# Low modes of 64 images: the table becomes the stationary operand and the images stream; one reload moves ahead of the last stores

## The reference, cut to what matters

```
xa_n = _inorm(xa, norm1_w, norm1_b)
k = _spec_conv(xa_n, kw1, kw2, (hk, wk))      # rfft2, 8x8 modes top and bottom, irfft2
q = _spec_conv(xa_n, qw1, qw2, (hk, wk))
v = _spec_conv(xa_n, vw1, vw2, (H, W))
dprod = softmax(einsum('batd,basd->bats', q, k) * sqrt(hk * wk))
att = einsum('bats,basd->batd', dprod, v)
att = _inorm(att, an_w, an_b) + xa
mix = _spec_conv(_inorm(att), mix_w1, mix_w2, (H, W))
```

## Time and profile before

| | us |
|---|---|
| median of 3 runs (lowest to highest) | 677.81 (675.39 to 679.09) |
| the profiled execution's own time | 681.9 |
| its span, first to last instruction | 679.9 |
| TensorE busy | 636.5 |
| VectorE busy | 487.8 |
| ScalarE busy | 334.3 |
| GpSimd busy | 356.1 |
| granted TensorE clock, mean | 0.984 of 2.4 GHz |

### The profile page before, as it was taken

How to read it: one execution, slowest core, us unless ns; L and a number is a source line. 1 busy time by engine, 2 the same in 40 slices (tenths; PEclk the granted TensorE clock), 3 DMA queues, 4 the chain that set the end, 5 groups by cost and what they waited for, 6 DMA issues and landing times.

```text
span 679.9 us, 15103 instructions
## 1 busy us (share of the span) xinstructions
PE 636.5 (94%) x5736; PEld 581.6 (86%) x5736; DVE 487.8 (72%) x1099; ACT 334.3 (49%) x722; POOL 356.1 (52%) x430
## 2 busy tenths in 40 slices
PE   9999999899999799979999899989999989995984
PEld 9999998699999799869999789969899988994863
DVE  4667676688777567668777666857887666778896
ACT  6888142465666413255666523246566650433331
POOL 0350035959960013796993002398799000359995
PEclk9999999899999899999999999999999989999997
DMA  9990000998999200299999900059989960004786
GB/s 320 350 379 9 1 2 20 308 314 294 310 318 328 94 1 1 77 308 343 286 328 309 322 14 1 2 198 331 321 285 325 308 218 1 1 1 162 280 302 247
DMA packets 72071, 136.32 MB, mean 200 GB/s; under 512 B 5760, under 2 KB 6272, under 8 KB 72000
## 3 DMA queue, kind: packets, MB, share of 16 engines
q1 hardware_dynamic: 72000, 135.36, 58.5%
HBM read 68.23 MB, written 67.11 MB: 199 GB/s over the span
## 4 chain that ended last, share of the span: by engine, by line
PE 58%; DVE 15%; POOL 9%; DMA 8%; issue 3%; ACT 3%; SPq 3%; POOLq 0%; DVEq 0%; ACTq 0%
PE psY L350 23%; PE psP L404 12%; POOL X L784 7%; PE psY L373 6%; DMA X<-in_x 6%; PE psT L389 5%; PE psP L454 5%; DVE QP L872 4%; ACT SQ L554 2%; PE psP L373 2%; DVE Y L836 2%; DVE SQ L836 2%; DMA out<-X 2%; SPq L318 2%; DVE X L836 1%
## 5 line engine op out<-in xcount | busy, mean ns | idle before, releaser
L350 PE MATMUL psY<-FWD,X 128*128 128x128 f32 x2048 | 251.1, 281 | 17.5 <-DMA X<-in_x 17.4
L350 PEld LDWEIGHTS psY<-FWD,X 128*128 128x128 f32 x2048 | 238.8, 195 | 33.0 <-issue 33.0
L784 POOL TENSOR_TENSOR X<-X,ALPHA 128x512 f32<-128x512 f32 x244 | 254.7, 1080 | 21.7 <-DVE IM L1072 19.7
L872 DVE TENSOR_REDUCE QP<-SQ 128x32 f32<-128x512 f32 x256 | 162.1, 679 | 57.8 <-ACT SQ L554 57.8
L836 DVE TENSOR_TENSOR X<-X,psP 128x512 f32<-128x512 f32 x192 | 126.5, 684 | 59.9 <-PE psP L404 26.1
L554 ACT ACTIVATE SQ<-X 128x512 f32<-128x512 f32 x256 | 146.4, 622 | 21.1 <-DMA X<-in_x 14.4
L404 PE MATMUL psP<-INVW,T 64*128 64x256 f32 x768 | 141.3, 402 | 12.0 <-DVE X L836 11.3
L762 POOL TENSOR_TENSOR Y<-Y,OMEGA 128x256 f32<-128x256 f32 x32 | 25.3, 790 | 215.9 <-ACT Y L558 215.6
L404 PEld LDWEIGHTS psP<-INVW,T 64*128 64x128 f32 x768 | 92.9, 190 | 31.2 <-issue 16.0
L576 ACT ACTIVATE T<-psT,BIA,SCL 128x256 f32<-128x256 f32 x128 | 65.3, 560 | 110.3 <-PE psT L389 105.8
L546 ACT ACTIVATE Y<-psY 128x512 f32<-128x512 f32 x128 | 76.2, 596 | 60.4 <-PE psY L350 59.6
(11 more groups left out here) (189 smaller groups left out, 478.8 us busy)
## 6 DMA issues: line engine op xcount, KB each, us to landing
X<-in_x SPq DMA_DIRECT2D x116, 512.0 KB, 5.5
out<-X SPq DMA_DIRECT2D x116, 512.0 KB, 4.4
X<-in_x SPq DMA_DIRECT2D x24, 256.0 KB, 5.2
out<-X SPq DMA_DIRECT2D x24, 256.0 KB, 3.7
INVH<-t_inv_h SPq DMA_DIRECT2D x1, 256.0 KB, 9.6
LW<-in_low_w SPq DMA_DIRECT2D x1, 204.0 KB, 6.6
GWT<-t_w SPq DMA_DIRECT2D x1, 192.0 KB, 9.9
FWD<-t_fwd SPq DMA_DIRECT2D x1, 128.0 KB, 2.1
```

Source lines behind the costliest of these rows:

```text
L350: last = mm(psY[p % 2][:, (2 * i + c) * 128:(2 * i + c + 1) * 128], X[:, 2 * p + i, a, c * 128:(c + 1) * 128], FWD[:, a, :], start=a == 0, ...
L784: P.tensor_tensor(v, v, al, MUL).then_inc(x_scaled, 1)
L872: V.tensor_reduce(QP[:, 4 * (k % 2) + place(n) % 4, :], SQ[:, n % RING, :].rearrange("p (a g j) -> p g a j", a=HC, j=GW), AX.XY, ADD).then ...
```

## The change

**Low modes.** For both k, the 64 columns of the table are now the stationary operand and 64 images times 8 values of u stream past it: 512 columns in one matmul, four matmuls (c, k), summed over c. k = 0 is written to partitions 0 to 63 and k = 1 to partitions 64 to 127 of one bank. u = 0 takes two matmuls of 64 columns. The result now has the table's columns on partitions, so it has to be turned: ScalarE copies it to SBUF (`ZT`, 128 by 512, and `ZT0`, 64 by 64), and nine matmuls with the copies as stationary operand and a new table MIRROR of ones, minus ones and zeros (32 columns) bring the images back on partitions and at the same time form the sums and differences for u and -u. The new table picks only the 8 values of v that are used. `modes(b, 0)` is split in two: its first half runs before the nine matmuls, its second half after them. VectorE then needs three plain copies instead of a copy, a copy, a sum and a difference. On ScalarE the two copies stand between the roots L600 and L602.

**SP's queue.** The reload of pair 29 now stands between the stores of pair 30 and of pair 31, and the reload of pair 30 comes right behind the stores of pair 31.

**Tables.** One more small table is loaded (16 KB), so 16 instead of 15 are counted.

```diff
@@ tables()
+    mirror = (row % 64 // 32 == col % 16 // 8) * (row % 32 == col % 8) * np.where(row // 64 * (col // 16) == 1, -1.0, 1.0)
@@ buffers
+        ZT, ZT0 = SQ[:, 0, :], SQ[0:64, 1, 0:IMGS]
@@ sync, batch(b, more)
-                for q in range(PAIRS - 2):
+                for q in range(PAIRS):
                     store(b, q)
                     if more and q:
                         reload(b + 1, q - 1)
-                for q in range(PAIRS - 2, PAIRS):
-                    store(b, q)
-                for q in range(PAIRS - 3, PAIRS) if more else ():
-                    reload(b + 1, q)
+                if more:
+                    reload(b + 1, PAIRS - 1)
@@ tensor, attend(b)
                 pe.wait_ge(scaled_w, 4 * b + 2)
-                for k, n in [(0, n) for n in range(1, 9)] + [(1, n) for n in range(1, 9)] + [(0, 0)]:
-                    ps, col = psZ[k if n else 2], 64 * max(n - 1, 0)
-                    if n == 0:
-                        pe.wait_ge(scaled_w, 4 * b + 4)
-                    for c in range(WC):
-                        last = mm(ps[0:IMGS, col:col + 64], Y[:, c, k, :, U0 + n], GWR[:, c, 0, k:k + 2, :],
-                                  start=c == 0, stop=c == WC - 1)
-                last.then_inc(z_made, 1)
-                modes(b, 0)
+                for c in range(WC):
+                    for k in range(2):
+                        last = mm(psZ[0][64 * k:64 * k + 64, :], GWR[:, c, 0, k:k + 2, :].rearrange("p r v -> p (r v)"),
+                                  Y[:, c, k, :, U0 + 1:U0 + 9], start=c == 0, stop=c == WC - 1)
+                last.then_inc(z_raw, 1)
+                pe.wait_ge(scaled_w, 4 * b + 4)
+                for c in range(WC):
+                    last = mm(psZ[1][0:64, 0:IMGS], GWR[:, c, 0, 0:2, :].rearrange("p r v -> p (r v)"),
+                              Y[:, c, 0, :, U0], start=c == 0, stop=c == WC - 1)
+                last.then_inc(z_raw, 1)
+                modes(b, 0, (0,))
+
+                pe.wait_ge(z_kept, 2 * b + 2)
+                for n in range(8):
+                    mm(psZ[2][0:IMGS, 32 * n:32 * (n + 1)], ZT[:, 64 * n:64 * (n + 1)], MIRROR[:, :],
+                       start=True, stop=True)
+                mm(psZ[2][0:IMGS, 256:272], ZT0, MIRROR[0:64, 0:16], start=True, stop=True).then_inc(z_made, 1)
+                modes(b, 0, (1,))
                 modes(b, 1)
@@ scalar, attend(b), between the roots L600 and L602
+                act.wait_ge(z_raw, 2 * b + 1)
+                nc.scalar.activation(ZT.rearrange("p (n i) -> p n i", n=8),
+                                     psZ[0][:, :].rearrange("p (i n) -> p n i", n=8), ACT.Copy).then_inc(z_kept, 1)
+                act.wait_ge(z_raw, 2 * b + 2)
+                nc.scalar.activation(ZT0, psZ[1][0:64, 0:IMGS], ACT.Copy).then_inc(z_kept, 1)
@@ vector, attend(b)
-                step(V.tensor_copy(sine, low_z(psZ[1], 8)))
-                do(V.tensor_copy(Xv[:, :, 8, :], low_z(psZ[2], 1)[:, 0, :, :]))
-                do(tt(Xv[:, :, 9:17, :], turned(low_z(psZ[0], 8)), turned(sine), ADD))
-                do(tt(Xv[:, :, 7::-1, :], turned(low_z(psZ[0], 8)), turned(sine), SUB))
+                low_z = psZ[2][0:IMGS, 0:256].rearrange("p (u s r v) -> p s r u v", s=2, r=2, v=LV)
+                do(V.tensor_copy(Xv[:, :, 8, :], psZ[2][0:IMGS, 256:272].rearrange("p (r v) -> p r v", r=2)))
+                do(V.tensor_copy(Xv[:, :, 9:17, :], low_z[:, 0, :, :, :]))
+                do(V.tensor_copy(Xv[:, :, 7::-1, :], low_z[:, 1, :, :, :]))
```

More of the change, by code:

```diff
@@ L15 @@
 PAIRS, QUADS, NG = IMGS // 2, IMGS // 4, IMGS // 8
-TABLES = 15
+TABLES = 16
 LAG = 3
@@ L68, in tables @@
                     + [p // 32 == i for i in range(4)], 1)
+    row, col = p[:, None], np.arange(32)[None, :]
+    mirror = (row % 64 // 32 == col % 16 // 8) * (row % 32 == col % 8) * np.where(row // 64 * (col // 16) == 1, -1.0, 1.0)
     f = lambda t: np.ascontiguousarray(t.reshape(t.shape[0], -1).astype(np.float32))
@@ L71, in tables @@
             "t_group": f(group_of), "t_eye": f(np.eye(IMGS)), "t_side": f(side), "t_pair": f(pair),
-            "t_rows": f(rows), "t_sel": f(p[:, None] % GROUPS == np.arange(GROUPS)[None, :])}
+            "t_mirror": f(mirror), "t_rows": f(rows), "t_sel": f(p[:, None] % GROUPS == np.arange(GROUPS)[None, :])}
 def spectral_block(nc, x, mix_re, mix_im, mix_mirror, low_w, low_mix, scalars,
-                   t_fwd, t_w, t_inv_h, t_inv_w, t_group, t_eye, t_side, t_pair, t_rows, t_sel, out):
+                   t_fwd, t_w, t_inv_h, t_inv_w, t_group, t_eye, t_side, t_pair, t_mirror, t_rows, t_sel, out):
     F32 = mybir.dt.float32
@@ L106, in spectral_block @@
         ROWS = sb("ROWS", [128, 10])
+        MIRROR = sb("MIRROR", [128, 32])
         SEL = sb("SEL", [128, GROUPS])
@@ L193, in spectral_block @@
         scaled_w = sem("scaled_w")
+        z_raw = sem("z_raw")
+        z_kept = sem("z_kept")
         z_made = sem("z_made")
@@ L310, in _ @@
                      (INVW[:, :], t_inv_w), (GROUP[:, :], t_group), (EYE[:, :], t_eye), (SEL[:, :], t_sel),
-                     (SIDE[:, :], t_side), (PAIR[:, :], t_pair), (ROWS[:, :], t_rows), (SC[:, :], scalars),
+                     (SIDE[:, :], t_side), (PAIR[:, :], t_pair), (ROWS[:, :], t_rows), (SC[:, :], scalars), (MIRROR[:, :], t_mirror),
                      (MRE, mix_re), (MIM, mix_im), (MMIR, mix_mirror), (flat(LM[:, :, :]), low_mix),
@@ L361, in add_squares, with modes @@
                 mm(psS[:, k:k + 1], quad, ONES[:, 0:1], start=True, stop=True).then_inc(q_added, 1)
-            def modes(b, q):
+            def modes(b, q, pairs=(0, 1)):
                 g = q // 2
@@ L367, in modes @@
                     pe.wait_ge(mode_weighted, 8 * b + g - 2)
-                for jj in range(2):
+                for jj in pairs:
                     col = 64 * (2 * (q % 2) + jj)
@@ L947, in attend @@
                 dve.wait_ge(z_made, b + 1)
-                low_z = lambda ps, n: ps[0:IMGS, 0:64 * n].rearrange("p (u r v) -> p u r v", r=2, v=NV)[:, :, :, 0:LV]
-                turned = lambda ap: ap.rearrange("p u r v -> p r u v")
-                sine = TMP[:, 0, 0, 0:128].rearrange("p (u r v) -> p u r v", r=2, v=LV)
-                step(V.tensor_copy(sine, low_z(psZ[1], 8)))
+                low_z = psZ[2][0:IMGS, 0:256].rearrange("p (u s r v) -> p s r u v", s=2, r=2, v=LV)
                 Xv = XL.rearrange("p r (u v) -> p r u v", v=LV)
-                do(V.tensor_copy(Xv[:, :, 8, :], low_z(psZ[2], 1)[:, 0, :, :]))
-                do(tt(Xv[:, :, 9:17, :], turned(low_z(psZ[0], 8)), turned(sine), ADD))
-                do(tt(Xv[:, :, 7::-1, :], turned(low_z(psZ[0], 8)), turned(sine), SUB))
+                do(V.tensor_copy(Xv[:, :, 8, :], psZ[2][0:IMGS, 256:272].rearrange("p (r v) -> p r v", r=2)))
+                do(V.tensor_copy(Xv[:, :, 9:17, :], low_z[:, 0, :, :, :]))
+                do(V.tensor_copy(Xv[:, :, 7::-1, :], low_z[:, 1, :, :, :]))
                 wait_link()
```

## The result

| | before | after |
|---|---|---|
| median of 4 runs, us (lowest to highest) | 678.45 (675.39 to 679.42) | 659.44 (657.47 to 661.40) |
| ratio, with its 95% interval | | 0.9695 (0.9651 to 0.9739) |
| span of the profiled execution | 679.9 | 655.5 |
| TensorE busy | 636.5 | 619.2 |

The kernel became 3.05% faster, 19.0 us between the medians. The profiled pair differs by more, 24.4 us of span, because that execution of before is slower than its median and this one of after is the fastest of its four.

A forecast was written before the change was run, and what follows sets the result against it. It took attend, hanging on the low modes, and the wait for pair 29's reload at batch ends as the bounds. 13.2 + 2.5 = 15.7 us off the 677.8 median gave 662.1, say 662 us; range 656 to 672.

The forecast's parts named there:

- The path: In attend, TensorE's and VectorE's paths run nearly level; both begin with the low modes, and all of attend hangs behind them.
- Low modes: predicted 13.2 us: In attend, scaling starts at 5.48 instead of 8.79 us: 3.3 us less a batch, times four.
- The one price left open: Long matmuls' moving read: runs of eight floats taken as contiguous, 0.46 us a pass, upper bound 0.90.
- the lone float in eight: Moving runs starting at an odd place: estimated 0.05 us more a pass, some 0.2 us a batch.
- Rival A: Low modes' long passes: column halves take turns, 1.84 us less gained a batch, 669.3 us in all; chance 27%.
- Rival B: Low modes' long passes: moving read slow and nothing overlaps, each batch loses 2.0 us, 683.3 in all; chance 8%.
- The overlap: Low modes' eight 512-column passes: two column halves run together, four slots, 1.84 us instead of 3.68.
- The queue: predicted 2.5 us: SP's new order at batch ends: net 0.8 us a boundary, three of them.
- I credit nothing for a clock that no longer falls: Batch ends: no gain counted for TensorE's clock staying up, though 16 passes had taken 3.35 instead of 2.02 us.
- the forward's gain of 1.0 an end: Batch ends: reload of pair 29 is issued earlier, gaining 0.65 to 1.7 us, lower end 0.2, taken as 1.0.
- what was to eat up to the whole 1.0 us at each end: Batch ends: pair 31's half stores leave 1.1 us later, so its last reload lands at 228.3 to 230.6.
- Rival C: SP's queue: new order gives back more than it brings, pair 31 late or clock falling, 669.1 us; chance 10%.

The follow-up runs named there:

- the kernel with one half: Changed kernel with both k written to the same column half, sine part left out; one execution, low modes to transposes 10.37 us.
- the second turning-first run: Changed kernel with both halves of modes 0 behind the nine turning matmuls, measured again: 658.66 us, ratio 0.9669 against the kernel before.

## Why the prediction was right, and where its sizes were off

**The whole.** Predicted were 15.7 us less and 662; measured were 19.0 less and 659.4 (19.8 less in the second measurement). The path was the one described: both sides of attend hang on the low modes, and the gain there passes through to the transposes undiminished. What is missing from the sum doesn't lie in attend (12.7 against 13.2) but mostly at the ends of the batches (7.3 in the profiled pair against 2.5).

**Low modes: predicted 13.2 us, by the traces 12.7.** Step by step, from the start of the low modes: long passes starting 0.49 us apart against 0.46; TensorE through with the first half of modes 0 at 3.6 against 3.31; the copies done at 2.9 against 2.95; VectorE's start 5.04 against 4.84; scaling 5.64 against 5.48; transposes 8.56 against 8.40. The one price left open, runs of eight at the price of contiguous, was 0.04 us a pair too low; the lone float in eight had been put at 0.05 and 0.2 us a batch, and 0.04 and 0.2 came. Rival A would have cost 1.84 a batch and costs 1.8 where it is forced; it did not come. Rival B needed 0.65 us a pass; a pass costs 0.48 with nothing overlapped. Its mechanism is real, though: single floats take 1.13 us a pair even with the halves overlapped, and that kernel's attend gains only 0.6 us a batch over before.

**The overlap rested on a thin row.** The prediction carried it over from L428's short loads to long column streams, and gave 27% to its failing. It came true, and the kernel with one half shows it. The order in the program, k inside c, turned out not to matter.

**The queue: predicted 2.5 us; against the kernel before it measured 8.0 (5.1 to 11.0), on top of the low modes 2.4 to 3.3 by the traces.** This is the term that was mis-sized. First, "I credit nothing for a clock that no longer falls": filling the wait in the kernel before brings 2.5 us, so there was something to credit. In the profiled pair it is 3.35 + 3.38 - 2 x 2.02 = 2.7 us. Second, the forward's gain of 1.0 an end. Against the kernel before, the queue alone cuts the idle time from 2.54, 3.23 and 2.60 to 0.64, 0.67 and 0.26 us, 2.3 an end. The changed kernel has 1.25, 1.40 and 0.94, 1.6 less an end; but with the low modes alone it is 1.77, 2.01 and 2.33, which leaves 0.8 an end to the queue. So the 1.0 is near where it was meant to hold, and what the sum lacked is that the ends get shorter with the low modes alone too (4.8 us in that one trace). Third, what was to eat up to the whole 1.0 us at each end ate nothing at batch 0. The half stores of pair 31 did leave later (213.44 and 213.98, 2.0 and 2.6 us after the first half store of pair 30, against 1.2 and 1.8), and the last reload left at 219.6, but it landed in 2.8 us, not in up to 5.2; all but one of the loads ahead of it had left 3.6 us or more before. It was in place at 222.4, and its forward, the last eight of the 32 passes from 220.48, came after it. At batch 1 TensorE waited 0.26 us for the first half of pair 31. Rival C, that the new order gives back more than it brings, is out.

**What stays open.** Why the ends are shorter with the low modes alone, under the old order of the queue, and whether they are in more than the one trace, no run shows; nor is it settled how the two edits share the 19 us, since the intervals of each are several us wide. In all kernels the stretch from the transposes to the last inverse transform, whose order of work no run here changes, takes 130.3 to 135.2 us, with long waits for the first reloads where it is long (3.09 us before one forward in the batch that took 135.2, in the second turning-first run). That alone spreads runs by a few us, and no run here says what sets it.

## What to carry to other kernels

Where a product's stationary side is strided and its result narrow, swap the sides: stream the large strided operand, hold the small table, put two such products in the two column halves, and pay for turning the result back only if the copy out of PSUM and the turning fit behind work that must be done anyway. Keep a moving operand's inner run at several floats (eight cost 0.04 us a pair here, single ones 0.64 more than that). When a queue is reordered at a stage's end, count an idle time of TensorE twice, once for itself and once for the clock that may fall behind it, and look for the load that is late next. And measure such an edit on top of the others as well as alone: here the two answers differ.

## What the runs showed of the hardware

- Two f32 streams of 512 columns with 128 rows and 64 stationary columns each overlap when they write different halves of the partitions: 0.49 us a pair against 0.48 for a single one, in both orders of the program that were tried. Two for the same half don't.
- The price of a moving read: one run of 512 floats 0.45 us a pair, runs of eight 0.49, single floats 64 apart 1.13.
- ScalarE's copy of 128x512 out of PSUM took 0.597 us with a stride of eight floats (row by line of the changed kernel below), the same as L546's without one.
- In the kernel before, the 16 passes behind idle times of 2.54 and 2.60 us took 3.35 and 3.38 us, the granted clock being 0.50 behind the first, and 2.02 behind one of 3.23; with the low modes alone they took 2.02 behind 1.77, 2.01 and 2.33. So the length of the idle time alone doesn't tell whether the clock falls.

```profile
L614 ACT ACTIVATE SQ<-psP x4: 597/597/597, 73.5 to 547.0; 128x512 f32<-128x512 f32 x4
```
